# Folding each head's squares twice on GpSimd in the steps without a value product

## The reference

```python
def rms_norm(x, w):
    var = jnp.mean(jnp.square(x), axis=-1, keepdims=True)
    return x * jax.lax.rsqrt(var + EPS) * w
qh = rms_norm((q @ Wq).reshape(b, l, 16, 64).transpose(0, 2, 1, 3), q_norm_w)
kh = rms_norm((kv @ Wk).reshape(b, s, 16, 64).transpose(0, 2, 1, 3), k_norm_w)
vh = (kv @ Wv).reshape(b, s, 16, 64).transpose(0, 2, 1, 3)
scores = jnp.where(mask, einsum('bhld,bhsd->bhls', qh, kh) / 8, -1e9)
o = einsum('bhls,bhsd->bhld', softmax(scores), vh)   # then @ Wo
```

## Time and profile before

| what | us |
|---|---|
| median of 3 runs (lowest, highest) | 2411.89 (2410.63, 2412.21) |
| the profiled execution's own time | 2413.2 |
| its span | 2411.4 |
| TensorE matmul busy | 2315.6 (96%) |
| VectorE busy | 2096.3 (87%) |
| ScalarE busy | 1364.6 (57%) |
| GpSimd busy | 1486.5 (62%) |

### The profile page before, as it was taken

The page is one execution under the profiler, slowest core; times in us unless marked ns, Lnnn a source line. Parts: engine busy times, 40 slices in busy tenths (PEclk is TensorE's granted clock), DMA queues, the critical chain, the costliest instruction groups (busy, mean ns, idle before and its releaser), DMA issues. The chain is left out here.

```text
span 2411.4 us, 57394 instructions
## 1 busy us (share of the span) xinstructions
PE 2315.6 (96%) x16343; PEld 1958.9 (81%) x16343; DVE 2096.3 (87%) x3379; ACT 1364.6 (57%) x2591; POOL 1486.5 (62%) x1069
## 2 busy tenths in 40 slices
PE   7988999999999999999999999999999999899985
PEld 4666888888888888888888888888888888788743
DVE  8788999999999999999999999999999997558776
ACT  5744555555555555555555555555555554355646
POOL 3546777777777777777777777777777772001100
PEclk9999999999999999999999999999999999999987
DMA  3431222222222222222222222222222214331000
GB/s 101 185 93 46 53 54 54 54 54 54 54 54 54 53 53 53 53 54 54 54 55 57 57 54 54 54 54 53 53 53 53 53 38 138 131 106 37 2 1 18
DMA packets 441099, 145.04 MB, mean 60 GB/s; under 512 B 365344, under 2 KB 423616, under 8 KB 440896
## 3 DMA queue, kind: packets, MB, share of 16 engines
q1 hardware_dynamic: 440880, 143.50, 24.0%
q10 hardware_dynamic: 144, 0.52, 0.1%
HBM read 109.17 MB, written 34.73 MB: 60 GB/s over the span
## 5 line engine op out<-in xcount | busy, mean ns | idle before, releaser
L456 POOL TENSOR_TENSOR probs<-arena,best_all 128x1024 f32 (+2 forms) x397 | 943.4, 2376 | 422.6 <-DVE best L833 401.3
L1085 PEld LDWEIGHTS u_ps<-rows,probs 128*128 128x128 f32 x6656 | 802.6, 192 | 57.1 <-issue 16.8
L1085 PE MATMUL u_ps<-rows,probs 128*128 (+1 forms) x6656 | 814.4, 276 | 9.9 <-ACT probs L661 5.0
L818 DVE SCALAR_TENSOR_TENSOR arena<-s_ps,mask,rrms 128x512 f32 (+2 forms) x832 | 603.8, 727 | 117.9 <-PE s_ps L962 116.1
L661 ACT ACTIVATE probs<-probs 128x1024 f32<-128x1024 f32 (+1 forms) x416 | 440.8, 1061 | 415.2 <-POOL probs L456 401.4
L793 DVE TENSOR_REDUCE ssq<-squares 128x16 f32<-128x1024 f32 (+2 forms) x416 | 490.4, 1179 | 38.0 <-ACT squares L619 36.7
L619 ACT ACTIVATE squares<-k_ps 128x512 f32<-128x512 f32 (+1 forms) x832 | 451.2, 591 | 43.5 <-PE k_ps L962 23.5
L833 DVE TENSOR_TENSOR best<-best,arena 128x1024 f32<-128x1024 f32 (+1 forms) x352 | 446.1, 1267 | 0.4 <-issue 0.2
L960 PE MATMUL k_ps<-w_hi,cT_hi 128*128 128x512 f32 (+1 forms) x832 | 362.5, 436 | 4.8 <-ACT squares L619 4.8
L613 ACT ACTIVATE cT_hi<-cT 128x128 fp32r<-128x128 f32 (+1 forms) x416 | 129.2, 311 | 368.5 <-DVE cT L784 368.5
L960 PE MATMUL s_ps<-q_hi,cT_hi 128*128 (+2 forms) x832 | 330.5, 397 | 3.3 <-DVE arena L818 3.0
(11 more groups left out here) (245 smaller groups left out, 2199.6 us busy)
## 6 DMA issues: line engine op xcount, KB each, us to landing
stage<-in_ctx SPq DMA_DIRECT2D x1536, 16.0 KB, 1.7
rows<-in_ctx SPq DMA_DIRECT2D x32, 768.0 KB
queries<-probs SPq DMA_DIRECT2D x16, 1024.0 KB, 4.0
q_plain<-queries SPq DMA_DIRECT2D x32, 512.0 KB, 3.3
best_all<-best_rows SPq DMA_DIRECT2D x31, 512.0 KB, 3.8
u_transposed<-uT_sb SPq DMA_DIRECT2D x124, 128.0 KB, 2.6
a_uT<-u_transposed SPq DMA_DIRECT2D x10, 1024.0 KB, 4.9
arena<-u_transposed SPq DMA_DIRECT2D x6, 1024.0 KB, 4.9
```

The costliest lines, as they stand in the source:

```text
L456: pool.tensor_tensor(probs[0:r, slot_of(c, PRING), :], scores_at(b, c), best_all[0:r, bass.ds((b % 2) * HL, HL)], ALU.subtract).then_inc(s ...
L818: dve.scalar_tensor_tensor(out=scores_at(p, c, h * HALF, HALF).rearrange("p (h l) -> p h l", l=L), in0=s_ps[h][0:r, :].rearrange("p (h l) ...
L1085: last = pe.matmul(u_ps[g // 3][:, at:at + UW], probs[0:r, s, g * P:(g + 1) * P], rows, start=(c == 0 and g % 3 == 0), stop=(c == NC - 1), ...
```

## The change

In steps 0 to 19 GpSimd folds twice: the 64 squares of a head to 32, written into half a slot of `probs` (slot 1, the halves in turn), and there, in place, the 32 to 16. VectorE sums 16 values a head from that half slot. `halved` now counts two for a step. ScalarE's squares of the next chunk wait for the first fold of this chunk and no longer for VectorE's sum. GpSimd's first fold waits for the even query stores, and from step 2 on each first fold waits for VectorE's sum of two steps before, which read the same half slot.

```diff
+        def folds(n, c, width):
+            at = (n % 2) * HALF
+            return probs[0:rows_of(c), 1, at:at + HALF].rearrange("p (h d) -> p h d", d=HD // 2)[:, :, 0:width]
...
             def fold_squares(n, c):
                 by_head = squares[0:rows_of(c), :].rearrange("p (h d) -> p h d", d=HD)
                 pool.wait_ge(squared.sem, squared.ended(n + KEYS_AHEAD))
-                low, high = by_head[:, :, 0:HD // 2], by_head[:, :, HD // 2:HD]
+                if n == 0:
+                    pool.wait_ge(q_stored[0], 8 * TILES)
+                if n >= 2:
+                    pool.wait_ge(summed.sem, summed.ended(n - 2 + KEYS_AHEAD))
+                half_sums = folds(n, c, HD // 2)
+                pool.tensor_tensor(half_sums, by_head[:, :, 0:HD // 2], by_head[:, :, HD // 2:HD], ALU.add).then_inc(halved, 1)
+                pool.wait_ge(halved, 2 * n + 1)
+                low, high = half_sums[:, :, 0:HD // 4], half_sums[:, :, HD // 4:HD // 2]
                 pool.tensor_tensor(low, low, high, ALU.add).then_inc(halved, 1)
...
-            def square(n, c, h):
-                if h == 0:
+            def square(n, c, h, last_folded):
+                if h == 0 and last_folded:
+                    act.wait_ge(halved, 2 * (n - 1 - KEYS_AHEAD) + 1)
+                elif h == 0:
                     act.wait_ge(summed.sem, summed.ended(n - 1))
...
-                        square(n + KEYS_AHEAD, at_step(p, c, KEYS_AHEAD)[1], h)
+                        square(n + KEYS_AHEAD, at_step(p, c, KEYS_AHEAD)[1], h, no_values(p, c - 1))
...
                 if folded:
-                    dve.wait_ge(halved, n - KEYS_AHEAD + 1)
+                    dve.wait_ge(halved, 2 * (n - KEYS_AHEAD) + 2)
+                    parts = folds(n - KEYS_AHEAD, c, HD // 4)
                 else:
                     dve.wait_ge(squared.sem, squared.ended(n))
-                width = HD // 2 if folded else HD
-                dve.tensor_reduce(ssq[0:r, c * H:(c + 1) * H],
-                                  squares[0:r, :].rearrange("p (h d) -> p h d", d=HD)[:, :, 0:width],
-                                  AX_X, ALU.add).then_inc(summed.sem, 1)
+                    parts = squares[0:r, :].rearrange("p (h d) -> p h d", d=HD)
+                dve.tensor_reduce(ssq[0:r, c * H:(c + 1) * H], parts, AX_X, ALU.add).then_inc(summed.sem, 1)
```

## The result

The changed kernel took 2416.13 us (median of 22 runs) beside 2410.58 of the kernel before on the same chips (22 runs): ratio 1.0023, 95% interval 1.0016 to 1.0029, so 5.6 us slower. The 20 steps without a value product hold the loss. These are their busy times in the changed kernel, from the first scaling of step 0 to that of step 20, and in a second execution of the same code; the columns are those of the earlier trace rows.

A forecast was written before the change was run, and what follows sets the result against it. VectorE, or a loop through it, bounds the 20 steps; GpSimd's folds and VectorE's maximum exclude each other. Laid out step by step, they sum to 79.46 us, +5.70, giving 2417.6 for the median; range 2411 to 2423.

The forecast's parts named there:

- sum of 256 elements: VectorE's sum of squares, 256 instead of 512 elements a partition: 0.40 us instead of 0.67, bounds 0.27 and 0.67.
- second fold: GpSimd's added fold of 256 elements a partition: 0.74 us, bounds 0.46 and 1.29.
- the distance from the end of the first fold to the second's start: GpSimd's wait on its own first fold before the second: 0.08 us.
- ordinary step: Steps 4 to 6: maximum, first fold and second fold form the loop, 3.54 us instead of 3.24, VectorE waiting 0.57.
- q_lo step: Steps 7 to 10, where GpSimd's q_lo holds the shared path behind the second fold and delays the maximum: 4.16 us.
- of the third kind: Steps with small operations between VectorE's sum and maximum; the first fold asks first: 4.66 to 5.26 us against 3.5 to 4.5.
- my rule of two operands: VectorE instructions with two SBUF inputs and GpSimd's SBUF reads exclude each other, first starter holding; VectorE's reductions and scalings exempt.
- Behind step 20 nothing changes: After the 20 steps touched by the diff, the kernel was expected to run as before, with no further gain or loss.
- hidden fold: Rival, chance 0.10: fold and maximum never wait for each other, steps 4–6 below 3.24 us each, 2408.8 us in all.
- cheap order: Rival, chance 0.18: fold-maximum race falls well, four steps with small operations cost +0.3 instead of about +0.95 each; 2415.0 us.
- clock's rival: Rival, chance 0.10: TensorE idles in the 20 steps and drops to half clock; four such steps add 8 us, 2425.

The follow-up runs named there:

- one-operand maximum: In both kernels, most maxima of steps 3 to 19 replaced by a one-operand reduction: changed kernel 73.50 us over 20 steps (1.0003), kernel before 73.03 (0.9984).
- half fold: Changed kernel with the second fold covering 8 of the 16 heads: 20 steps 75.23 us, ratio 0.9999 to the kernel before.
- one fold: Changed kernel without the second fold, VectorE summing 32 values a head again: 20 steps 74.36 us, ratio 0.9994 to the kernel before.
- squares that wait: Changed kernel, but ScalarE's squares wait for VectorE's sum as in the kernel before: 20 steps 82.62 us, ratio 1.0044 to the kernel before.
- sum of 32: Changed kernel, but VectorE sums 32 values a head after both folds: 20 steps 84.59 us, ratio 1.0039 to the kernel before.
- no second fold with q_lo: Changed kernel without the second fold in steps 7 to 10, VectorE summing 32 values there: 20 steps 76.98 us, ratio 1.0029 to the kernel before.

## Why the prediction was right, and where it wasn't

**The result.** Forecast +5.7 us, measured +5.6 (ratio 1.0023).

**The terms.** The sum of 256 elements takes 0.40 behind other work and 0.42 after a wait (0.40 assumed); the second fold 0.74 (0.74); the distance from the end of the first fold to the second's start is 150.57 - 150.48 = 0.09 (0.08).

**The ordinary step.** 3.54 forecast, 3.53 to 3.55 in all six (steps 4 to 6 of two profiles). The one-operand maximum shows the cause (2.97 without the exclusion), the half fold the price (0.27 for 0.28). VectorE's idle time is 0.48 and not 0.57; the other 0.09 is the overlap with the instruction before, which a sum that has waited doesn't get.

**The q_lo step.** 4.16 forecast; steps 8 and 9 took 4.17 and 4.16 in the first profile and 4.16 twice in the second.

**By groups**, against the second profile: steps 0–3 14.80 forecast, 14.77 measured; 4–6 10.62, 10.61; 7–12 24.87, 24.99; 13–14 7.27, 7.37; 15–18 16.53, 16.73; step 19 5.37, 5.35. The sum was 0.36 us short.

**What was wrong inside it.** The steps "of the third kind" are right in number and their sum nearly in length, but their working was not. I had the small operations merely delay the maximum. In fact they are themselves caught, the mean of squares too, which has one operand in SBUF:

```profile
139.67 1.28 POOL L502 TENSOR_TENSOR probs<-squares 128x512 f32<-128x512 f32 x1
139.77 1.24 DVE L813 TENSOR_SCALAR ms<-ssq 128x80 f32<-128x80 f32 x1
...
192.00 2.53 POOL L502 TENSOR_TENSOR probs<-squares 128x512 f32<-128x512 f32 x1 [0.51 <-ACT squares L633]
192.08 0.18 DVE L813 TENSOR_SCALAR ms<-ssq 128x80 f32<-128x80 f32 x1
192.19 1.21 DVE L846 TENSOR_TENSOR best<-best,arena 128x1024 f32<-128x1024 f32 x1
...
196.31 1.21 DVE L69 TENSOR_TENSOR tmp<-y 128x80 f32<-128x80 f32 x1
197.54 0.78 DVE L71 SCALAR_TENSOR_TENSOR tmp<-tmp,ms 128x80 f32<-128x80 f32 x1
```

In step 2 the fold is recorded 0.10 us ahead of the mean of squares, and the mean waits for it. In step 15 it is recorded 0.08 ahead and loses: the mean takes 0.18, the maximum behind it its 1.21, and the fold lasts 2.53, through both. In step 16 two Newton steps are caught, one behind each fold. So steps 15 and 16 are 3.68 and 6.34 and not 4.66 and 5.16; the pair's sum, 10.02, is near the forecast 9.82 by luck rather than by reason. The Trainium skill, page "SBUF — State Buffer", section "Who interferes with whom", says that `tensor_scalar` can enter a mode with two ports and then contends; the 1.24 agrees, and my rule of two operands was too narrow.

**"Behind step 20 nothing changes".** Right for the order of work, not for the clock. From the scaling of step 20 to that of step 23 the kernel before took 15.2 us and the changed one 13.6 in both profiles. The granted clock over the 13.6 us behind step 20 is 0.87 there and 1.00 here. But it isn't bound to the change: the other kernels above fall into 13.6 (one fold, squares that wait, half fold) and 15.0 to 15.3 (both one-operand maxima, sum of 32, no second fold with q_lo).

**The rivals.** The hidden fold is refuted by 3.54 in the steps 4 to 6. The cheap order, where fold and maximum would come apart in the steps of the third kind, did not happen. The clock's rival happened in small: one dip in step 12 to 13, 0.9 us in one of two executions, not 8. Its price was also worked out too high: products of 6.3 us at half the clock are 2 more than a q_lo step of 4.16 gives, but only 1 more than the longest step named, 5.26.

## What to carry to other kernels

Before work is moved from VectorE to GpSimd, add up what both do on the path that they share: GpSimd's two-input instructions and VectorE's two-operand instructions (and, as seen here, a `tensor_scalar`) of a step, as if they were one engine. Here that sum went from 2.78 to 3.48 us a step while VectorE's own work went from 3.24 to 2.97, and the larger of the two nearly set the step (3.54, and 3.24 before). A short instruction that shares the path with a long one can cost the long one's whole length.

## What the runs showed of the hardware that I had not expected

Races are decided by hundredths of a microsecond, and the recorded starts don't tell to the last of them who wins. The fold at 151.69, after a maximum at 151.68, waited 1.06 us. A fold recorded 0.10 us ahead of the mean of squares won (139.67 and 139.77). One recorded 0.08 ahead won in the changed kernel with the one-operand maximum (184.79 and 184.87) and lost in the changed kernel (192.00 and 192.08), where it then waited for the maximum of 192.19 as well. A `tensor_scalar` over 80 elements of one SBUF operand lasted 1.24 and 1.27 us behind a fold, 0.18 where it went first, while a `tensor_reduce` over 1024 elements (1.21) and a fold (1.30) ran side by side. And an unaltered stretch of TensorE's work, the end of the preparation and the first value product, comes in two lengths (the first scaling of step 0 starts between 130.7 and 132.3 us in seven of the ten profiles here and between 134.3 and 135.3 in three; the granted clock tells them apart, 0.99 against 0.96 up to there). What decides which one an execution gets stays open.
